# Handing on the two score banks of a windowed attention one by one, with a new weaving table, in a four-layer kernel on one Trainium2 core

## The chip, the core and the metric

One Trainium2 chip, of which the kernel uses one core. The engines are PE (TensorE: matmuls, with PEld for its weight loads), ACT (ScalarE), DVE (VectorE), POOL (GpSimd) and the DMA queues, issued from SP. Times are device microseconds of one launch; lower is better.

## The reference, cut to what matters

The input holds 8 sequences of 512 tokens and 128 channels. Each goes through four layers of the form x = x + s * silu(f), where s is an attention-like branch and f a feed-forward branch, both of the layer norm of x. Layer 1's f is the part that the change touches: a depth-2 stack in which every block does

```
q, k = l2norm(q) * qs, l2norm(k) * ksc;  q, k = rotary_xpos(q, k)
sim = where((i < j) | (i > j + 64), -big, 8 * q @ k.T)      # 8 heads of 64, window of 64
o = softmax(sim) @ v;  x = x + o @ wo
x = x + (a * gelu(g)) @ w2 + b2      # a, g from the layer norm of the shifted x
```

Layer 0 is a delta-rule scan beside a chain of small networks, layer 2 a state scan beside four experts, and layer 3 an attention whose softmax keeps the 25 largest of 512 scores in each row, found by repeated searches for the 8 largest. All arithmetic is in fp32.

## The kernel before, in words

Channels lie on the 128 partitions and tokens along the free axis. Layers 0, 1 and 2 of a sequence are one stream of work, called the item. Layer 3 of the sequence before it is a second stream, the search. The program is nine blocks: one with an item alone, seven passes of a loop in which the item of sequence b runs beside the search of sequence b-1, and one with a search alone.

Each engine has a queue that it works off in order. The four queues are written by generators that yield at the same places: the item has 200 steps, the search some 264. `weave(a, b)` merges the two: after step n of the item it puts as many steps of the search as digit n of the string `SEARCH` says (base 36). The same string orders all four engines, so it is the only scheduler; there is no dynamic one.

Steps 1 to 24 of the search set layer 3 up. Then come 32 pairs of rows of scores, 7 steps each, numbered 25 to 248, and in each of them DVE does two searches over 128x512: either two MAX8 (L2036) or two MATCH_REPLACE8 (L2040). The last 16 steps hold work of PE, ACT and POOL alone.

Layer 1's attention (the helpers `score`, `turn`, `exponent`, `take_turned`, `largest`, `share`, `divide`) has 8 units in each of the 2 blocks of the stack: unit n is 128 queries (q = n // 2) and four of the eight heads. Its scores are 4 x 192 columns in two PSUM banks, A[0] and A[1], two heads in each. A unit goes like this. PE writes the mask and the scores to both banks (`score`). DVE takes the row maxima of both in one TENSOR_REDUCE (L1189) and multiplies them by the norm of the query (L1192, "shift"). ACT computes four exponents with their sums (L1072), two from each bank. DVE takes reciprocals of the sums (L1201), and POOL multiplies the probabilities by them (L1295). PE transposes them to bank A[2], one half (e = 0, 1) at a time (`turn`, L925), and ACT copies each half out (L1083). Then PE multiplies by the values into A[3].

The units are pipelined by one: on PE, unit n's part is scores of n+1, turn of (n, 0), [at0], turn of (n, 1), [at1], values of n, [at2], where the names in brackets are the yields. On ACT it is copy of (n, 0), [at0], copy of (n, 1), the four exponents of n+1, [at1], and an output copy of every second unit, [at2]. On DVE it is maxima and shift of n+1, [at0], both reciprocals, [at1], [at2]. The scores of n+1 wait for the exponents of both banks of n, since they overwrite both.

Tables of ACT's functions are loaded where the next function in its queue needs another set (L309).

Of the kernel before, what the change touches and what calls it, by code (L numbers as in the profile page):

```python
# [8 lines left out]
ALU = mybir.AluOpType  # L9
# [194 lines left out]
class Layer:  # L204
# [9 lines left out]
    def __call__(self, name, count):  # L214
# [5 lines left out]
SEARCH = ("0030001012121031111222010302030140211310211202111220023121011011011112100401413120420311233210122111"  # L220
          "0013220130010120201016010416010130221000200144026030a2025106024101006010033015100000200010101000252")
# [11 lines left out]
def build(nc, x_in, w_in, c_in, e_in, out, wcols, ccols, ecols):  # L233
# [5 lines left out]
    with ctx:  # L239
# [420 lines left out]
        def names(*tables):  # L660
# [13 lines left out]
            PE="pj 16,px 16,mix_xc 2,mix_var 2,k 2,v 2,r 2,wo 2,ss_q 2,ss 8,vp 8,score 16,turned 32,pv 16,attn 2,gp 6,ap 6,ffn_out 2",  # L674
            ACT="hs_a 2,sqq 16,mix_sq 2,mix_ln 2,mix_rs 2,k_sb 2,sr 2,q_ln 2,q_rs 2,rn_ln 8,rn 8,vt 8,exp 32,pt 32,of 8,hs2_a 2,"
                "gelu 6,gate 1",
            DVE="t1 16,t2 16,mix_g 2,mix 2,kv 2,state 2,y 2,h 2,qk 8,qrs 2,max 16,shift 16,rec 32,x1 2,gg 6,x2 2,hs_0 1,hs_b 2,hs2_b 2,m 1,x_new 1",
# [180 lines left out]
        def l1_pe(pe):  # L858
# [45 lines left out]
            def score(i, n):  # L904
                q, f = n // 2, n % 2
                lo = 128 * q - WIN if q else 0
                n0 = 0 if q else WIN
                halves = [A[e].rearrange("p (s j) -> p s j", s=2)[:, :, n0:KW] for e in range(2)]
                for e in range(2):
                    mm(halves[e], eye[:], band[:, None, n0:KW].to_broadcast([128, 2, KW - n0]), True, False)  # L910
                for s in range(2):
                    for e in range(2):
                        g = 2 * f + s
                        r = mm(halves[e][:, s], L.qk[64 * e:64 * e + 64, g * T + 128 * q:g * T + 128 * q + 128],
                               L.qk[64 * e:64 * e + 64, (4 + g) * T + lo:(4 + g) * T + 128 * q + 128], False, s == 1)
                r.then_inc(S["score"], 1)
# [12 lines left out]
            for i in range(DEPTH):  # L929
# [31 lines left out]
                score(i, 0)  # L961
# [49 lines left out]
        def l1_act(a):  # L1011
# [21 lines left out]
            def query_root(i):  # L1033
# [3 lines left out]
                if i:  # L1037
                    a.wait_ge(*S("shift", NU * i))
# [20 lines left out]
            def exponent(i, n):  # L1059
                q, f, k = n // 2, n % 2, NU * i + n  # L1060
                n0 = 0 if q else WIN
                a.wait_ge(*S("shift", k + 1))
                if n == 0:
                    a.wait_ge(*S("zero", 2) if i == 0 else S("t3", 4 * (i + 1)))
                if k >= 2:
                    a.wait_ge(*S("turned", 2 * (k - 1)))
                    a.wait_ge(*S("rec", 2 * (k - 1)))
                table(LN, TANH)
                for e in range(2):
                    for s in range(2):  # L1070
                        j = 2 * e + s
                        r = act(L.probs[f][:, j, WIN + n0:256], A[e][:, 256 * s + n0:256 * s + KW], ACT.Exp,  # L1072
                                scale=L.qrs[:, 2 * f + s, q, e:e + 1], bias=L.shift[f][:, j:j + 1],
                                accum_out=L.zsum[f][:, j:j + 1])
                    r.then_inc(S["exp"], 1)
# [9 lines left out]
            for i in range(DEPTH):  # L1085
# [27 lines left out]
                exponent(i, 0)  # L1113
# [34 lines left out]
        def l1_dve(v):  # L1148
# [26 lines left out]
            def turn(i, n):  # L1175
# [3 lines left out]
                if n == 4 and i:  # L1179
                    v.wait_ge(*S("score", NU * i))  # L1180
                stt(L.qk[:, n * T:(n + 1) * T], L.rn[n % 2], 1e12, L.t1[n % 2], ALU.min, ALU.mult).then_inc(S["qk"], 1)

            def largest(i, n):
                q, f, k = n // 2, n % 2, NU * i + n
                n0 = 0 if q else WIN
                v.wait_ge(*S("score", k + 1))
                if k >= 2:
                    v.wait_ge(*S("exp", 2 * (k - 1)))
# [1050 lines left out]
```

## Time and profile before

| | |
|---|---|
| median of 3 runs | 5378.93 us (5370.84 to 5409.69) |
| profiled execution, its own time | 5400.17 us |
| span of the profiled execution | 5398.3 us |
| mean granted TensorE clock | 0.793 |
| DVE busy | 4012.1 us, 74% of the span |
| PE busy | 4091.9 us, 76% |
| ACT busy | 2922.0 us, 54% |
| POOL busy | 2520.7 us, 47% |
| HBM traffic | 7 GB/s |

A window of the trace is a stretch of the span, counted from its start. The row of a window gives, for each engine, how long it was busy and with how many instructions, and then the clock that TensorE was granted as a share of full speed. What is left between an engine's busy time and the length of the window is idle.

### The profile page before, as it was taken

To read this page: it belongs to the slowest core of one execution; us is meant where nothing else is said; L and a number is where in the kernel's file an instruction comes from. 1 tells how busy PE (TensorE), PEld (TensorE's weight loads), DVE (VectorE), ACT (ScalarE), POOL (GpSimd) and SP (SyncE) were. 2 spreads that over 40 slices of the span, in tenths; PEclk is the share of its full clock that TensorE was granted. 3 is DMA by queue.
4 is the path that set the end of the run, shared out by engine and by line. 5 is a ranking of instruction groups with operands and counts; after the bars stand their busy time and mean duration, and the time that the engine had idled before them with its cause. 6 is when DMAs were issued, how large, how long until landed. Compare 5 with 4: busy or idle time off the path is not lost. (4 is left out here: it accounts for less than half of the span.)

```text
span 5398.3 us, 58321 instructions
## 1 busy us (share of the span) xinstructions
PE 4091.9 (76%) x16660; PEld 1894.8 (35%) x16660; DVE 4012.1 (74%) x7871; ACT 2922.0 (54%) x5717; POOL 2520.7 (47%) x2324
## 2 busy tenths in 40 slices
PE   5776877768777787877878688786877768787676
PEld 1332334323443234422443234432344323442233
DVE  3325688876878678885787867887788867888598
ACT  3443566545555465655555465654556545565343
POOL 1114355444545345462553625545355544546265
PEclk8876898868887788968888688886898778986555
DMA  1000000000000000000000000000000000000000
GB/s 78 1 24 2 2 1 24 1 3 2 1 24 1 3 3 1 24 0 3 3 1 24 3 3 1 24 1 3 2 1 24 1 3 3 1 24 1 2 1 3
DMA packets 7995, 44.07 MB, mean 8 GB/s; under 512 B 848, under 2 KB 848, under 8 KB 7248
## 3 DMA queue, kind: packets, MB, share of 16 engines
q1 hardware_dynamic: 7632, 39.89, 1.9%
q8 instruction: 148, 2.42, 0.2%
q14 instruction: 215, 1.76, 0.1%
HBM read 37.52 MB, written 2.36 MB: 7 GB/s over the span
## 5 line engine op out<-in xcount | busy, mean ns | idle before, releaser
L2036 DVE MAX8 m<-top 128x8 f32<-128x512 f32 x2048 | 1292.5, 679 | 3.1 <-ACT top L1966 2.6
L2102 POOL TENSOR_SCALAR top<-top,m 128x512 f32<-128x512 f32 x512 | 813.6, 1589 | 959.0 <-DVE m L2036 834.4
L2040 DVE MATCH_REPLACE8 top<-m,top 128x512 f32<-128x512 f32 x1536 | 1026.1, 675 | 0.3
L288 PE MATMUL bank<-arena,consts 128*128 128x512 f32 (+1 forms) x912 | 624.7, 779 | 114.8 <-ACT arena L406 42.3
L2108 POOL TENSOR_TENSOR top<-top 128x512 f32<-128x512 f32 x512 | 656.0, 1281 | 20.2 <-ACT top L1974 2.4
L288 PE MATMUL bank<-arena,weights 128*128 128x512 f32 (+8 forms) x976 | 536.8, 669 | 87.3 <-issue 20.7
L1901 PE MATMUL bank<-consts,top 128*128 128x128 f32 x2048 | 417.6, 340 | 192.7 <-POOL top L2108 137.6
L288 PE MATMUL bank<-arena 128*64 128x128 f32 (+3 forms) x3200 | 474.5, 371 | 44.9 <-ACT arena L1083 40.2
L1901 PEld LDWEIGHTS bank<-consts,top 128*128 128x128 f32 x2048 | 303.8, 175 | 477.7 <-POOL top L2108 282.7
L1981 ACT ACTIVATE top<-bank 128x512 f32<-128x512 f32 x512 | 305.6, 597 | 298.0 <-PE bank L1901 297.4
L288 PE MATMUL bank<-top,vt 128*9 128x128 f32 x4096 | 344.0, 323 | 141.4 <-ACT top L1981 141.4
L1966 ACT ACTIVATE top<-bank 128x512 f32<-128x512 f32 x512 | 302.7, 593 | 225.4 <-PE bank L288 163.6
L1642 POOL TENSOR_TENSOR arena<-arena 128x1024 f32<-128x1024 f32 x128 | 287.0, 2242 | 210.3 <-DVE arena L1611 207.6
L309 ACT ACT_TABLE_LOAD x294 | 377.2, 1283 | 5.2
L288 PE MATMUL bank<-kf,qm 32*128 32x512 f32 x1024 | 373.6, 813 | 3.2 <-ACT top L1966 3.2
L1974 ACT ACTIVATE top<-top,nmx 128x512 f32<-128x512 f32 x512 | 365.3, 721 | 0.9
L1295 POOL TENSOR_TENSOR arena<-arena 128x384 f32<-128x384 f32 (+1 forms) x256 | 197.5, 775 | 340.9 <-DVE arena L1201 340.8
L288 PEld LDWEIGHTS bank<-arena 128*64 128x64 f32 (+2 forms) x3200 | 277.4, 181 | 215.1 <-issue 166.2
L820 POOL TENSOR_TENSOR arena<-arena,hold 128x512 f32<-128x512 f32 x64 | 83.7, 1308 | 539.2 <-DVE arena L793 539.1
L288 PE MATMUL bank<-hold,weights 128*128 128x512 f32 (+2 forms) x512 | 303.8, 725 | 24.3 <-DVE hold L427 5.6
L288 PEld LDWEIGHTS bank<-arena,consts 128*128 128x128 f32 (+1 forms) x912 | 190.8, 235 | 363.4 <-issue 134.1
L288 PEld LDWEIGHTS bank<-arena,weights 128*128 128x128 f32 (+5 forms) x976 | 175.3, 201 | 398.8 <-issue 197.1
(287 smaller groups left out, 6636.4 us busy)
## 6 DMA issues: line engine op xcount, KB each, us to landing
arena<-experts_dram SPq DMA_DIRECT2D x32, 768.0 KB, 7.1
weights<-weights_dram SPq DMA_DIRECT2D x1, 6982.0 KB, 19.2
hold<-x_dram SPq DMA_DIRECT2D x9, 256.0 KB, 2.7
out_dram<-x_out SPq DMA_DIRECT2D x9, 256.0 KB, 3.4
consts<-consts_dram SPq DMA_DIRECT2D x1, 1759.5 KB, 23.6
rot<-consts_dram SPq DMA_DIRECT2D x1, 1024.0 KB, 25.6
```

What stands on the lines that cost most here:

```text
L288: return nc.tensor.matmul(o, lhsT, rhs, start=start, stop=stop)
L309: nc.scalar.preload_act_table_set(name)
L1295: nc.gpsimd.tensor_tensor(p, p, L.rec[f][:, 2 * e:2 * e + 2, None].to_broadcast([128, 2, KW - n0]), ALU.mult).then_inc(S["shared"], 1)
L1642: nc.gpsimd.tensor_tensor(L.hc[n % 2], L.hh[n % 2], L.cn[n % 3][:, None, :].to_broadcast([128, 2, T]), ALU.mult).then_inc(S["hc"], 1)
L1901: i = nc.tensor.transpose(Y[:, 128 * k:128 * k + 128], pp[e][:, 128 * k:128 * k + 128], C("ident"))
L1966: act(sc[slot(p, e)], X[e], ACT.Copy).then_inc(SB["sc"], 1)
L1974: act(ex[e], sc[slot(p, e)], ACT.Exp, scale=SC, bias=nmx[:, slot(p, e):slot(p, e) + 1], accum_out=zs[:, q, heads[e]:heads[e] + 1]).then_in ...
L1981: act(pt_[e], Y, ACT.Copy).then_inc(SB["pt"], 1)
L2036: nc.vector.max(m8[:, slot(p, e), k], src).then_inc(SB["top"], 1)
L2040: nc.vector.match_replace(wk_[e], m8[:, slot(p, e), k], sc[slot(p, e)] if k == 0 else wk_[e], -3e38).then_inc(SB["rest"], 1)
L2102: nc.gpsimd.tensor_scalar(pp[e], sc[slot(p, e)], m8[:, slot(p, e), TOPK // 8, 0:1], None, ALU.is_ge).then_inc(SB["kept"], 1)
L2108: nc.gpsimd.tensor_tensor(pp[e], pp[e], ex[e], ALU.mult).then_inc(SB["pp"], 1)
```

## The change

Every hand-over between PE, DVE and ACT in this attention is split by bank. `score`, `largest`, `exponent` and `share` get an argument e, and the semaphores score, max and shift count 32 instead of 16. Two score matmul groups, two maxima, two shifts and two pairs of exponents take the place of one, one, one and four exponents together. A bank's scores now wait for the exponents of that bank alone, and its exponents for its own shift. The queues are reordered:

```diff
 PE:
-                        pe.wait_ge(*S("exp", 2 * k + 2))
-                        score(i, n + 1)
+                        score(i, n + 1, 0)
                     turn(i, n, 0)
                     yield "at0"
+                    if n + 1 < NU:
+                        score(i, n + 1, 1)
                     turn(i, n, 1)
                     yield "at1"
 ACT:
+                    if n + 1 < NU:
+                        exponent(i, n + 1, 0)
                     take_turned(i, n, 0)
                     yield "at0"
+                    if n + 1 < NU:
+                        exponent(i, n + 1, 1)
                     take_turned(i, n, 1)
-                    if n + 1 < NU:
-                        exponent(i, n + 1)
                     yield "at1"
 DVE:
                     if n + 1 < NU:
-                        largest(i, n + 1)
+                        largest(i, n + 1, 0)
                     yield "at0"
                     if n + 1 < NU:
-                        share(i, n + 1)
+                        share(i, n + 1, 0)
+                        largest(i, n + 1, 1)
                     yield "at1"
+                    if n + 1 < NU:
+                        share(i, n + 1, 1)
                     yield "at2"
 largest:
-                nc.vector.tensor_reduce(L.nmax[f], banks[:, 0:2].rearrange("p b (s j) -> p (b s) j", s=2)[:, :, n0:KW],
+                nc.vector.tensor_reduce(L.nmax[f][:, 2 * e:2 * e + 2], A[e].rearrange("p (s j) -> p s j", s=2)[:, :, n0:KW],
 score:
+                if n:
+                    pe.wait_ge(*S("exp", 2 * k + e - 1))
```

The matmuls, exponents, reciprocals and POOL's operations keep their shapes and counts. And the string changes as a whole:

```diff
-SEARCH = ("0030001012121031111222010302030140211310211202111220023121011011011112100401413120420311233210122111"
-          "0013220130010120201016010416010130221000200144026030a2025106024101006010033015100000200010101000252")
+SEARCH = ("0010002001010111011132020561620320302221222111023010011000003101002001201400230111110120322150031110"
+          "0230211111210121310064000451706132515220431001312252515343003223011000200000200010000100110001010221")
```

Item steps 0 to 32 are layer 0, 33 to 132 layer 1 (its two attentions are steps 48 to 73 and 96 to 121, in 8 units of at0, at1, at2 after two steps of opening), and 133 to 199 layer 2.

## Rows read from the trace of the kernel before

**Rows 1.** The page, section 1: busy time, share of the span, instructions.
```profile
PE 4091.9 (76%) x16660; PEld 1894.8 (35%) x16660; DVE 4012.1 (74%) x7871; ACT 2922.0 (54%) x5717; POOL 2520.7 (47%) x2324
```
**Rows 2.** Windows: the item alone, one loop pass, the search alone.
```profile
core 0: us, PE busy (x) PEld busy (x) DVE busy (x) ACT busy (x) POOL busy (x), PEclk, DMA share, GB/s
0.00:529.80 529.80, 360.41 (x1093) 155.69 (x1093) 199.66 (x303) 210.37 (x402) 115.67 (x99) 0.78 0.07 26
...
2455.50:3097.40 641.90, 504.87 (x2082) 235.04 (x2082) 500.78 (x981) 365.14 (x715) 315.07 (x290) 0.81 0.02 6
...
5023.10:5398.30 375.20, 244.01 (x994) 111.77 (x994) 304.95 (x701) 154.69 (x310) 197.74 (x196) 0.52 0.01 2
```
**Rows 3.** Windows: stages of that loop pass, in order.
```profile
2479.90:2565.20 85.30, 70.97 (x170) 25.14 (x168) 57.20 (x94) 53.06 (x82) 24.97 (x22) 0.90 0.00 0
...
2576.70:2623.20 46.50, 43.35 (x161) 20.38 (x160) 38.00 (x73) 27.09 (x49) 23.09 (x20) 0.89 0.00 1
2623.20:2690.70 67.50, 52.60 (x362) 31.53 (x362) 47.19 (x115) 39.65 (x116) 36.81 (x41) 0.80 0.00 1
2690.70:2717.20 26.50, 20.77 (x102) 9.58 (x102) 25.46 (x60) 16.35 (x30) 13.26 (x13) 0.94 0.00 1
...
2772.50:2837.90 65.40, 49.18 (x368) 30.71 (x366) 50.63 (x126) 40.89 (x119) 40.25 (x46) 0.87 0.00 1
2837.90:2868.30 30.40, 24.18 (x78) 10.10 (x78) 22.47 (x47) 16.76 (x27) 13.45 (x13) 0.72 0.28 104
...
2870.90:2893.60 22.70, 15.80 (x56) 7.71 (x56) 18.28 (x45) 14.62 (x23) 6.12 (x8) 0.71 0.00 0
2893.60:2974.20 80.60, 71.83 (x294) 35.04 (x294) 65.23 (x142) 43.86 (x74) 35.11 (x36) 0.89 0.00 1
2974.20:2996.90 22.70, 17.45 (x71) 7.11 (x71) 21.04 (x46) 17.46 (x34) 13.35 (x13) 0.76 0.00 0
2996.90:3084.40 87.50, 57.43 (x162) 21.23 (x161) 80.00 (x102) 41.76 (x72) 68.77 (x45) 0.58 0.00 0
```
**Rows 4.** Windows: the same stages with no search beside them (first block).
```profile
164.20:223.00 58.80, 40.01 (x246) 24.70 (x246) 11.09 (x33) 26.35 (x84) 12.38 (x16) 0.74 0.00 1
223.00:241.30 18.30, 13.29 (x22) 4.69 (x22) 4.67 (x8) 5.88 (x8) 0.00 (x0) 0.81 0.00 1
282.30:338.90 56.60, 36.93 (x246) 22.68 (x246) 11.09 (x32) 26.24 (x84) 12.38 (x16) 0.79 0.00 0
...
359.40:380.20 20.80, 12.70 (x28) 5.82 (x28) 8.24 (x21) 10.87 (x14) 0.14 (x2) 0.58 0.00 0
...
445.10:513.70 68.60, 44.48 (x62) 11.30 (x61) 58.18 (x50) 31.50 (x48) 51.20 (x29) 0.50 0.00 0
```
**Rows 5.** Timeline of one unit with no search beside it, second attention.
```profile
311.77 0.50 PE L288 MATMUL bank<-band,eye 128*128 128x384 bf16 x2 [0.88 <-ACT arena L1072]
...
313.17 0.96 DVE L1189 TENSOR_REDUCE arena<-bank 128x4 f32<-128x768 f32 x1 [1.25 <-PE bank L288]
...
314.16 0.16 DVE L1192 TENSOR_TENSOR arena<-arena 128x4 f32<-128x4 f32 x1
...
315.15 0.60 ACT L1083 ACTIVATE arena<-bank 128x512 f32<-128x512 f32 x1 [0.81 <-PE bank L925]
315.65 0.51 ACT L1072 ACTIVATE arena<-bank,arena 128x192 f32<-128x192 f32 x1
...
315.89 1.09 PE L288 MATMUL bank<-arena 128*64 128x128 f32 x16 [0.78 <-ACT arena L1083]
...
317.78 0.50 PE L288 MATMUL bank<-band,eye 128*128 128x384 bf16 x2 [0.79 <-ACT arena L1072]
```
**Rows 6.** Groups by line and form, second attention of the loop pass (2772.5:2837.9).
```profile
L2036 DVE MAX8 m<-top 128x8 f32<-128x512 f32 x36 | 22.8, 679 | 0.0
...
L1189 DVE TENSOR_REDUCE arena<-bank 128x4 f32<-128x768 f32 x6 | 5.7, 950 | 2.1 <-PE bank L288 2.1
...
L1072 ACT ACTIVATE arena<-bank,arena 128x128 f32<-128x128 f32 x8 | 3.6, 462 | 1.5 <-DVE arena L1192 1.5
...
L1189 DVE TENSOR_REDUCE arena<-bank 128x4 f32<-128x512 f32 x2 | 1.4, 678 | 0.0
```
**Rows 7.** The page, section 5: loads of ACT's function tables.
```profile
L309 ACT ACT_TABLE_LOAD x294 | 377.2, 1283 | 5.2
```

More of the change, by code:

```diff
@@ L673, in build @@
         S1 = marks.layer(**names(norm_names(("xn", False), ("ffn0", True), ("ffn1", True)), dict(
-            PE="pj 16,px 16,mix_xc 2,mix_var 2,k 2,v 2,r 2,wo 2,ss_q 2,ss 8,vp 8,score 16,turned 32,pv 16,attn 2,gp 6,ap 6,ffn_out 2",
+            PE="pj 16,px 16,mix_xc 2,mix_var 2,k 2,v 2,r 2,wo 2,ss_q 2,ss 8,vp 8,score 32,turned 32,pv 16,attn 2,gp 6,ap 6,ffn_out 2",
             ACT="hs_a 2,sqq 16,mix_sq 2,mix_ln 2,mix_rs 2,k_sb 2,sr 2,q_ln 2,q_rs 2,rn_ln 8,rn 8,vt 8,exp 32,pt 32,of 8,hs2_a 2,"
                 "gelu 6,gate 1",
-            DVE="t1 16,t2 16,mix_g 2,mix 2,kv 2,state 2,y 2,h 2,qk 8,qrs 2,max 16,shift 16,rec 32,x1 2,gg 6,x2 2,hs_0 1,hs_b 2,hs2_b 2,m 1,x_new 1",
+            DVE="t1 16,t2 16,mix_g 2,mix 2,kv 2,state 2,y 2,h 2,qk 8,qrs 2,max 32,shift 32,rec 32,x1 2,gg 6,x2 2,hs_0 1,hs_b 2,hs2_b 2,m 1,x_new 1",
             POOL="zero 2,q_sb 8,t3 8,shared 32")))
@@ L902, in value, with score @@
                 mm(A[q % 2], L.hs[:, 128 * q:128 * q + 128], W(f"l1_qkv{i}", lo=1024)).then_inc(S["vp"], 1)
-            def score(i, n):
-                q, f = n // 2, n % 2
+            def score(i, n, e):
+                q, f, k = n // 2, n % 2, NU * i + n
                 lo = 128 * q - WIN if q else 0
                 n0 = 0 if q else WIN
-                halves = [A[e].rearrange("p (s j) -> p s j", s=2)[:, :, n0:KW] for e in range(2)]
-                for e in range(2):
-                    mm(halves[e], eye[:], band[:, None, n0:KW].to_broadcast([128, 2, KW - n0]), True, False)
+                half = A[e].rearrange("p (s j) -> p s j", s=2)[:, :, n0:KW]
+                if n:
+                    pe.wait_ge(*S("exp", 2 * k + e - 1))
+                mm(half, eye[:], band[:, None, n0:KW].to_broadcast([128, 2, KW - n0]), True, False)
                 for s in range(2):
[L912 to L915, printed above, removed]
+                    g = 2 * f + s
+                    r = mm(half[:, s], L.qk[64 * e:64 * e + 64, g * T + 128 * q:g * T + 128 * q + 128],
+                           L.qk[64 * e:64 * e + 64, (4 + g) * T + lo:(4 + g) * T + 128 * q + 128], False, s == 1)
                 r.then_inc(S["score"], 1)
@@ L960, in l1_pe @@
                 pe.wait_ge(*S("qk", 4 * (i + 1)))
-                score(i, 0)
+                score(i, 0, 0)
+                score(i, 0, 1)
                 yield "hop"
@@ L1037, in query_root @@
                 if i:
-                    a.wait_ge(*S("shift", NU * i))
+                    a.wait_ge(*S("shift", 2 * NU * i))
                 act(flat, A[3][:, 0:32], ACT.Ln, scale=NORM_SCALE, bias=C("floor")).then_inc(S["q_ln"], 1)
@@ L1057, in fetch_v, with exponent @@
                 act(L.vt[:, q], A[q % 2].rearrange("p (h d) -> p h d", d=DH), ACT.Copy).then_inc(S["vt"], 1)
-            def exponent(i, n):
+            def exponent(i, n, e):
                 q, f, k = n // 2, n % 2, NU * i + n
                 n0 = 0 if q else WIN
-                a.wait_ge(*S("shift", k + 1))
+                table(LN, TANH)
+                a.wait_ge(*S("shift", 2 * k + e + 1))
                 if n == 0:
@@ L1065, in exponent @@
                 if k >= 2:
[L1066 to L1075, printed above, removed]
+                    a.wait_ge(*S("turned", 2 * (k - 2) + e + 1))
+                    a.wait_ge(*S("rec", 2 * (k - 2) + e + 1))
+                for s in range(2):
+                    j = 2 * e + s
+                    r = act(L.probs[f][:, j, WIN + n0:256], A[e][:, 256 * s + n0:256 * s + KW], ACT.Exp,
+                            scale=L.qrs[:, 2 * f + s, q, e:e + 1], bias=L.shift[f][:, j:j + 1],
+                            accum_out=L.zsum[f][:, j:j + 1])
+                r.then_inc(S["exp"], 1)
             def take_turned(i, n, e):
@@ L1232, in l1_dve @@
                 v.wait_ge(*S("qrs", i + 1))
-                largest(i, 0)
+                largest(i, 0, 0)
+                largest(i, 0, 1)
                 yield "hop"
-                share(i, 0)
+                share(i, 0, 0)
+                share(i, 0, 1)
                 yield "hop"
@@ L1282, in l1_pool @@
                             if n == 0 and i:
-                                g.wait_ge(*S("score", NU * i))
+                                g.wait_ge(*S("score", 2 * NU * i))
                             nc.gpsimd.tensor_tensor(L.qk[:, n * T:(n + 1) * T], L.t1[n % 2], L.t2[n % 2],
```

28 lines of the change are left out of this document (14 added, 14 removed).

## The prediction

> **What bounds the kernel now.** I read the page's busy times first: DVE 74% and PE 76% busy, ACT 54%, POOL 47% [rows 1]. No engine is full, so the mean says little. The windows by block say where the time is: seven loop passes of 641.9 us, 4493 of 5398 us. In one, DVE is busy 501 us, PE 505 us [rows 2]. Then I cut a pass into stages at DVE's own instructions and set the woven stages [rows 3] beside the same stages of the first block, which has no search [rows 4]. The reader is to see two kinds of stage. Some are full on DVE: the feed-forward of the first stack block (25.5 busy of 26.5 us), the state scan (80.0 of 87.5). In others DVE has room while the item's own chain runs: layer 0 (57.2 of 85.3), the two attentions (47.2 of 67.5 and 50.6 of 65.4), the experts (65.2 of 80.6) [rows 3]. The attention takes 58.8 and 56.6 us alone [rows 4], so its 29 and 31 search steps lengthen it by only 8.7 and 8.8 us: some 0.3 us for a step that keeps DVE busy for 1.28 us (my sum: 50.6 less about 12 of the attention's own, over 31; two MAX8 of 0.68 overlap a little [rows 6]). Attention is bound by its chain, and the search fills the gaps.
>
> **Part 1, the chain of a unit.** In the unit alone, at full clock, one mask matmul to the next is 317.78 - 311.77 = 6.01 us [rows 5]. It is made of scores (to the turn at about 1.3), turn, copy, turn, copy (to 315.65, when exponents start) and four exponents (2.1). The maxima end at 314.13 and the shift at 314.32, but the exponents begin at 315.65: ACT was still copying. So DVE is **not** on this loop; it has 1.33 us to spare [rows 5].
>
> Now the new order. Counting from the first mask matmul: a bank's scores end at about 0.85 (half of the group, with the pipeline's end). The maxima of one bank cover 384 columns. No row has that form; 768 columns take 0.95 and 512 take 0.678 [rows 6], a slope of 1.06 ns a column, which gives 0.54 for 384. It can't be above the 0.68 of 512 columns, and half of 0.95 is the least; I take 0.54, on the line through both forms. Shift 0.16, with hand-overs: exponents of bank 0 from 1.6 to 2.6. The copy of (n, 0) stands behind them on ACT, to 3.2. DVE's queue has the reciprocal of bank 0, which waits for these exponents, ahead of the maxima of bank 1: they run from 2.85 to 3.4, the shift to 3.55, exponents of bank 1 from 3.6 to 4.6, copy of (n, 1) to 5.2. The values (1.09 [rows 5]) wait for this copy, and on PE's queue the next scores of bank 0 stand behind the values: 5.2 + 1.1 = 6.3. So the period is about 6.25 us against 6.01: what is won by working on two banks at once is paid back, because the values, which ran beside the exponents before, are now in series, and so are maxima and shift. With PE at 1.2 GHz (the clock granted to these stages is 0.80 and 0.87 of full [rows 3], so part of the time) the same count gives 8.05, and the old order needs 8.0 by PE's groups at double length. I take **+0.25 us a unit**, between -0.1 and +0.5.
>
> DVE's own work grows by one fixed part of a maximum (0.95 becomes 2 x 0.54, +0.13) and one shift (+0.16): 0.3 us a unit, inside its idle time alone, but in the sum where DVE is full.
>
> The Trainium skill ("VectorE: DVE Perf Modes", the section on the TRN2 errata) speaks against splitting: PSUM-source operations cost 120 cycles at 0.96 GHz plus one a column, so 125 ns are paid again with each part. By the two forms above it is 0.13. In the whole program it would be 16 us by the page and 17 by the trace, of DVE's time, not of the path: 16 units in each of 8 blocks.
>
> **Part 2, the table.** I counted the digits of both strings between the item steps at which my stages begin and end; only search steps 25 to 248 hold DVE work, and both sums are 224. Steps before -> after, and the change of the stage in us, at 1.28 us of DVE a step:
> - Layer 0, 10 -> 17: 9 us of DVE into 28 idle, but in bursts of 6 at its end (digits 5, 6, 1, 6), where DVE is full. +5 (0 to 9).
> - Layer 0's end to layer 1's shift, 7 -> 5: full on DVE, -2.6. Projections, 15 -> 18, 38.0 of 46.5 busy: +2 (0 to 3.8).
> - First attention, 29 -> 21: 8 steps fewer at 0.3 to 1.28, not below 58.8 alone [rows 4]: -5; eight units of part 1, +2. Together **-3** (-8 to +2).
> - First feed-forward, 16 -> 9: DVE 25.5 - 9.0 = 16.5, alone 18.3 [rows 4], so 19.9: -6.6. The step behind it, 2 -> 1: -1.3. Second projections, 19 -> 19: 0.
> - Second attention, 31 -> 36: 5 steps at 0.3 to 1.28, +4, eight units, +2: **+6** (+1 to +9). Ten of the 36 stand in the last unit, where nothing of the attention hides them.
> - Second feed-forward, 13 -> 23: DVE 22.5 + 12.8 = 35.3, and 3 idle: +8 (5 to 12).
> - Layer 2's opening and router, 8 -> 20: DVE 18.3 + 15.4 = 33.7, and 2 idle: +13 (11 to 17).
> - Experts, 41 -> 42, and ACT's table loads in a pass: following the functions through both orders by hand I count 38 before (7 x 38 and the ends make up the 294 of [rows 7]) and 40 after, two more of these here, 1.28 us each: +1 (-5 to +5). Behind the experts, 14 -> 12: -1.5.
> - State scan, 18 -> 0: DVE 80.0 - 23.0 = 57, and alone it takes 68.6 [rows 4], which then holds it, with TensorE granted 0.50 of its clock alone and 0.58 beside the search: -18 (-19 to -15).
>
> The sum is 5 - 2.6 + 2 - 3 - 6.6 - 1.3 + 6 + 8 + 13 + 1 - 1.5 - 18 = **+2 us a pass**, +14 for seven. The first block has 16 units at 0.25: +4. The last block has no attention. So 5398.3 + 18 = 5416 of span, and the profiled execution's 5400.2 becomes 5418. That execution lies 21 us above the median, so on the median: 5379 + 18 = **5397 us**. What the sum says in plain words: the table takes the search out of a full stage (the scan) and puts it into stages that become full by it.
>
> No DMA is moved; the experts' weights are issued after the second attention as before and have 30 us.
>
> **The rivals.**
> (A) The split pays in the woven state. Alone, units cannot use more, but beside the search PE and ACT also do its matmuls and copies (PE 52.6 and ACT 39.7 busy of 67.5 [rows 3]), and smaller hand-overs let these slip between. At best DVE or PE bound the attentions: the second at 50.6 + 6.4 + 2.4 = 59.4 and little idle, 61; the first at PE's 52.6 less what 8 steps have, about 56 with hand-overs. That is 15 less instead of +3 for both, so 18 to 19 less a pass. Half of it, as is likelier, gives 5397 - 7 x 9.5 = **5330 us**; all of it 5267. For it: 20 and 15 us of idle DVE in these stages, the largest room there is. Against it: the order of part 1 puts copies behind exponents that wait for DVE.
> (B) DVE comes onto the unit's loop. Before, exponents waited 1.5 us in a whole attention for the shift [rows 6], thanks to the 1.33 us to spare. Now maxima are needed at once, and a search step that stands ahead of them delays the whole loop by up to 1.28 us, twice a unit. Half of one step a unit is 0.64 x 16 = 10 us a pass: 5397 + 72 = **5469 us**. It decides from the point where the mean wait for the shift passes some 0.6 us a unit; then the result is slower.
> (C) The stages that become full don't fill. The experts, with 41 steps, leave DVE idle for 15.4 us, 0.37 a step [rows 3]. If the 22 steps put into the second feed-forward and the router cost that on top, it is +8 a pass: **5454 us**.
> (D) The change doesn't overlap what it says, because in a woven queue the exponents of bank 0 end before the scores of bank 1 are issued anyway. Then part 1 is +0.3 of DVE work and no more; it is in the forecast's range.
>
> **How the numbers follow.** Forecast, with (D): 0.40. (A): 0.27. (B): 0.21. (C): 0.12. Within 1% (54 us, about what a measurement of this kernel can tell from no change) is the forecast alone, 0.40; faster 0.27; slower 0.33. The forecast's own range, from the bounds of the stages, is 5397 with some 6 us a pass either way, 5355 to 5440. The range of all reaches to most of (A), 5267 being its end, and past (B) and (C): 5270 to 5490.
>
> **What would show it.** Part 1: in the first block the attentions stay within 3 us of 58.8 and 56.6; (A) would have them under 55 or the woven ones at 61 and 56. Part 2: the scan near 69.5 us with TensorE granted half its clock, the router stage near 36, the second feed-forward near 38, the second attention near 71, and 294 + 14 = 308 table loads. (B): L1072 waits for L1192 for over 5 us in an attention. (C): idle DVE of over 5 us in the router and second feed-forward stages. The prediction is wrong if layer 0 loses more than 9 us to its bursts, or if the woven attentions leave the bounds of -8 to +9.

## The result and the profile after

The changed kernel takes 5614.67 us (median of 4, 5606.48 to 5644.02) against 5382.08 us before in the same comparison: a ratio of **1.043** [1.038, 1.049]. The forecast was 5397, some 18 us more than before, with a range up to 5490. The sign was right, but the loss is 233 us, thirteen times the forecast one and outside the range. The profiled span went from 5398.3 to 5604.7, 206 us more.

The page after: busy times, then three groups (the last two numbers are the idle time ahead of the group and what ended most of it).

```profile
PE 4301.8 (77%) x16660; PEld 2094.3 (37%) x16660; DVE 4035.9 (72%) x8127; ACT 2956.3 (53%) x5731; POOL 2531.5 (45%) x2324
...
L1073 ACT ACTIVATE arena<-bank,arena 128x192 f32<-128x192 f32 (+1 forms) x512 | 249.9, 493 | 488.6 <-DVE arena L1196 488.6
...
L1193 DVE TENSOR_REDUCE arena<-bank 128x2 f32<-128x384 f32 (+1 forms) x256 | 133.6, 522 | 400.5 <-PE bank L288 396.5
...
L309 ACT ACT_TABLE_LOAD x308 | 395.2, 1283 | 5.6
```

DVE and ACT do about what they did [rows 1]; the table loads are the 308 that I counted. What is new is one wait: the exponents (L1073) stand 488.6 us for DVE's shift (L1196), 3.8 us a unit over 128 units. Before, the wait was 1.5 us in a whole attention [rows 6]. PE is busy 210 us more with the same 16660 instructions.

Windows of the trace after: the first block's attentions, alone; then, from one loop pass of the changed kernel, layer 0, the first attention, second attention, second feed-forward, layer 2's opening and router, experts, scan.

```profile
165.40:241.60 76.20, 61.21 (x249) 39.64 (x248) 14.07 (x50) 26.56 (x85) 12.38 (x16) 0.53 0.00 0
304.30:379.60 75.30, 61.06 (x250) 40.16 (x248) 13.90 (x49) 26.54 (x84) 12.37 (x16) 0.52 0.00 1
...
2579.10:2678.80 99.70, 80.42 (x204) 27.88 (x203) 67.95 (x124) 56.21 (x91) 29.83 (x28) 0.87 0.00 0
...
2731.50:2810.20 78.70, 65.12 (x333) 43.15 (x332) 39.66 (x109) 36.50 (x108) 30.35 (x34) 0.65 0.00 1
...
2882.70:2977.20 94.50, 81.88 (x391) 52.57 (x390) 59.06 (x156) 45.13 (x128) 44.04 (x47) 0.58 0.00 1
2977.20:3010.70 33.50, 25.15 (x127) 11.10 (x128) 33.20 (x75) 21.04 (x36) 20.29 (x22) 0.91 0.25 95
3014.60:3049.20 34.60, 24.18 (x110) 11.81 (x108) 34.08 (x79) 21.62 (x38) 18.46 (x20) 0.70 0.00 1
3049.20:3121.80 72.60, 65.98 (x297) 33.47 (x298) 66.25 (x147) 46.88 (x76) 33.93 (x35) 0.98 0.00 1
3144.00:3215.30 71.30, 42.33 (x90) 13.81 (x91) 62.99 (x55) 33.62 (x52) 56.31 (x32) 0.64 0.00 0
```

The seven loop passes took 641.9 us each before and 665.8 after (529.8 to 5023.1, and 569.1 to 5229.4 us of the span). Cut at the same instructions and averaged over the passes:

```
stage                        before   after   change   forecast
layer 0                        86.2   101.1    +14.9       +5
layer 0's end                  11.5     7.6     -3.9       -2.6
projections, first             46.5    45.9     -0.6       +2
first attention                64.6    80.2    +15.6       -3
first feed-forward + step      29.6    23.6     -6.0       -7.9
projections, second            52.3    48.8     -3.5        0
second attention               65.2    86.2    +21.0       +6
second feed-forward            28.2    33.4     +5.2       +8
layer 2's opening, router      21.5    34.7    +13.2      +13
experts                        80.6    72.5     -8.1       +1
behind the experts             22.6    20.6     -2.0       -1.5
scan                           87.5    71.4    -16.1      -18
the rest                       45.6    39.8     -5.8        -
```

The two attentions give 36.6 us more a pass, everything else together 12.7 less. Alone, with no search and so no table in play, they went from 58.8 and 56.6 [rows 4] to 76.2 and 75.3. So at least that part has nothing to do with the search steps.

The timeline of one unit alone, after (start, length, instruction, then the idle time before it and its releaser), set beside [rows 5]:

```profile
320.17 0.50 PE L288 MATMUL bank<-band,eye 128*128 128x384 bf16 x1
...
320.60 1.65 PE L288 MATMUL bank<-arena 64*128 64x192 f32 x4
...
322.18 1.11 PE L925 MATMUL bank<-consts,arena 128*128 128x128 f32 x4
322.28 0.56 DVE L1193 TENSOR_REDUCE arena<-bank 128x2 f32<-128x384 f32 x1 [3.30 <-PE bank L288]
...
323.07 0.51 ACT L1073 ACTIVATE arena<-bank,arena 128x192 f32<-128x192 f32 x1 [2.19 <-DVE arena L1196]
323.08 0.53 PE L288 MATMUL bank<-band,eye 128*128 128x384 bf16 x1
...
323.54 1.65 PE L288 MATMUL bank<-arena 64*128 64x192 f32 x4
...
325.12 1.12 PE L925 MATMUL bank<-consts,arena 128*128 128x128 f32 x4
325.22 0.56 DVE L1193 TENSOR_REDUCE arena<-bank 128x2 f32<-128x384 f32 x1 [0.86 <-PE bank L288]
...
326.01 0.51 ACT L1073 ACTIVATE arena<-bank,arena 128x192 f32<-128x192 f32 x1 [1.36 <-DVE arena L1196]
...
327.00 0.59 ACT L1084 ACTIVATE arena<-bank 128x512 f32<-128x512 f32 x1
...
327.74 1.98 PE L288 MATMUL bank<-arena 128*64 128x128 f32 x16 [1.50 <-ACT arena L1084]
...
329.65 0.50 PE L288 MATMUL bank<-band,eye 128*128 128x384 bf16 x1
```

From mask to mask it is 9.48 us (320.17 to 329.65), and the rows are one chain: bank 0's scores and the turn behind them on PE (2.91), bank 1's mask and scores (2.14), maxima and shift (0.79), two exponents (0.99), the copy (0.74), the values (1.91). Read the copy: its input, the second turn, was done at 325.12 + 1.12 = 326.24, but it starts at 327.00, behind exponents that had themselves waited for DVE until 326.01. PE idles 1.50 us for it, then does the values, and the next scores stand behind these. DVE's reciprocal isn't a link of this chain: DVE has done it and then idles 0.86 us until PE has written bank 1. The Trainium skill ("TensorE: Matmul & The Clock Gate", "Architectural detail: the array is 16× 32×32, not 1× 128×128") calls ACT and DVE strictly first in, first out; the row agrees, a copy whose data was there did not pass the exponents. The mask takes 0.50 us for one bank, as two banks took in [rows 5]: this unit runs at 1.2 GHz. The windows of these attentions are granted 0.53 and 0.52, where it was 0.74 and 0.79 [rows 4].

### The profile page after: what moved, and what is told of

Read it like the earlier page. It is cut to its first block and busy times, and to the rows that moved or that the text cites. A ratio compares the mean times of both kernels' runs of the same rounds, so it can differ in the third digit from the quotient of the medians.

```text
span 5604.7 us, 58831 instructions
## 1 busy us (share of the span) xinstructions
PE 4301.8 (77%) x16660; PEld 2094.3 (37%) x16660; DVE 4035.9 (72%) x8127; ACT 2956.3 (53%) x5731; POOL 2531.5 (45%) x2324
## 5 line engine op out<-in xcount | busy, mean ns | idle before, releaser
L288 PE MATMUL bank<-arena 128*64 128x128 f32 (+3 forms) x3200 | 727.7, 444 | 142.3 <-ACT arena L1084 142.3
L288 PE MATMUL bank<-arena,consts 128*128 128x512 f32 (+1 forms) x912 | 611.1, 763 | 94.5 <-POOL arena L1650 27.3
L288 PEld LDWEIGHTS bank<-arena 128*64 128x64 f32 (+2 forms) x3200 | 463.3, 224 | 348.0 <-issue 262.7
L1073 ACT ACTIVATE arena<-bank,arena 128x192 f32<-128x192 f32 (+1 forms) x512 | 249.9, 493 | 488.6 <-DVE arena L1196 488.6
L1193 DVE TENSOR_REDUCE arena<-bank 128x2 f32<-128x384 f32 (+1 forms) x256 | 133.6, 522 | 400.5 <-PE bank L288 396.5
L288 PE MATMUL bank<-hold,weights 128*128 128x512 f32 (+2 forms) x512 | 271.7, 656 | 81.2 <-DVE hold L643 26.2
```

The costliest lines, as they stand in the source:

```text
L288: return nc.tensor.matmul(o, lhsT, rhs, start=start, stop=stop)
```

## The experiments

Three theories. **Q**: the queue orders put copies and maxima behind exponents, so that one long loop forms through ACT, DVE and PE. **P**: PE's scores lose the pairing of the two row halves when each bank is written by itself. **T**: the new table. Later **K**: TensorE's lower clock is a loss of its own. The first four kernels take P and T.

**Scores in bank order, kernel before.**

```diff
-                for s in range(2):
-                    for e in range(2):
+                for e in range(2):
+                    for s in range(2):
```


> The kernel before, and only the order of a unit's eight score matmuls is changed: all of bank 0 (rows 0 to 63 of the array), then all of bank 1 (rows 64 to 127), where they alternated. Theory P (matmuls of the two row halves ran two at a time, and the change undid that): a unit's 8 row-tiled score instructions take about 3.3 us at half clock instead of 1.65, the attentions of the first block go from 58.8 and 56.6 us to 70 to 76, TensorE's clock in them falls towards 0.5, and the time rises by 3 to 4%, to some 5570 us. Theory O (the new queue order costs: values, maxima and shift in series): no change, 5382 within 0.5%, since no queue order between engines is touched. Theory T (the new table costs): no change either.

Measured: 5389.35 us, 1.002 [1.0006, 1.0034]; attentions alone 56.5 and 55.8. The timeline of this kernel shows why:

```profile
311.49 0.93 PE L288 MATMUL bank<-arena 64*128 64x192 f32 x8
```

All eight score instructions still take 0.93 us; in the trace those of the two halves start 13 to 14 ns apart (the first two at 311.491 and 311.505), though four of one half stand ahead of four of the other in the queue. The order inside a group costs nothing as long as both banks are there.

**Both banks' scores issued together, in the changed kernel** (its other edits kept).

```diff
-                        score(i, n + 1, 0)
+                        score(i, n + 1)          # both banks, halves alternating
                     turn(i, n, 0)
                     yield "at0"
-                    if n + 1 < NU:
-                        score(i, n + 1, 1)
```


> The changed kernel, but the scores of both banks of a unit are issued together again, alternating between the row halves, when the exponents of both banks before are done; maxima, shifts, exponents and reciprocals stay split by bank, in the new order, with the new table. Theory P: the attentions of the first block return to 59 to 64 us (the split's own order costs 0.25 us a unit), their clock to 0.7 to 0.8, and the time is 5330 (5280 to 5400) us, 1% under the kernel before, since the new table outside the attentions saves 12 us a pass. Theory O: the attentions stay at 72 to 76 us alone and the time above 5520. Theory T: above 5500.

Measured: 5617.03, 1.045 [1.0428, 1.0472]; attentions alone 73.8 and 73.7. PE's busy time in them fell from 61 to 47 us, and the time stayed: P is real work for PE and not the cause. What holds the chain changed: a unit takes 9.11 us at half clock (313.60 to 322.71), and now the second maxima start at 318.03, right behind the reciprocal at 317.95, with both banks' scores done since 316.

**The two tables, crossed** (the string alone is exchanged): the changed kernel with the old string, and the kernel before with the new one.

> The changed kernel with the old weaving table. Theory P: the attentions alone are the same as with the new table (76 and 75 us) and the time is no better than the changed kernel's, 5640 to 5720 us, because the stages outside the attentions lose the 12 us a pass that the new table gave. Theory T: the loss goes away, under 5450 us.

> The kernel before with the new weaving table: only the digits change. Theory P with my reading of the stages: woven attentions at about 60 and 70 us, the rest of a pass at 500, so 630 us a pass instead of 642 and 5300 us (5250 to 5360) in all, faster than the kernel before by 1.5%. Theory T: slower than before, above 5450 us.

Measured: 5675.52, 1.055 [1.0521, 1.0576], and 5393.1, 1.0022 [1.0004, 1.004]. T falls too: with the old attention the new table makes a pass of 641.3 us against 641.9. It moves time (layer 0 +13, router +14, scan -16, experts -8) and saves none. In the changed kernel it softens the loss by 61 us. The difference lies in the woven attentions: with the old attention the table makes the two 8.2 us a pass longer (64.6 and 65.2 become 68.3 and 69.7), with the changed one 2.9 us shorter (84.3 and 85.1 become 80.2 and 86.2).

**The split alone.** The hand-overs are split by bank as in the change; the queues keep the old order (both maxima, both reciprocals; both copies, then the four exponents; both banks' scores together), old table.

```diff
 ACT:
                     take_turned(i, n, 1)
                     if n + 1 < NU:
-                        exponent(i, n + 1)
+                        exponent(i, n + 1, 0)
+                        exponent(i, n + 1, 1)
 DVE:
-                        largest(i, n + 1)
+                        largest(i, n + 1, 0)
+                        largest(i, n + 1, 1)
                     yield "at0"
-                        share(i, n + 1)
+                        share(i, n + 1, 0)
+                        share(i, n + 1, 1)
```


> The kernel before, old table, with only the hand-overs split by bank: maxima, shifts, exponents and reciprocals of a bank each, with semaphores of their own, but every queue in the order of before (both maxima; copy, copy, four exponents; both reciprocals) and the scores of both banks issued together. Theory Q (what costs is the new order of the queues, exponents ahead of copies): 5382 us within 0.7%, attentions of the first block at 56 to 60 us. Rival S (the split itself costs, by more and smaller instructions and more semaphores): attentions over 64 us alone, time above 5430 us.

Measured: 5389.45, 1.001 [0.9997, 1.0022]; alone 57.2 and 58.8. The finer semaphores, 128 more maxima and as many shifts cost nothing that shows.

**The changed kernel with one swap on ACT**, new table.

```diff
-                        exponent(i, n + 1, 0)
                     take_turned(i, n, 0)
+                        exponent(i, n + 1, 0)
                     yield "at0"
-                        exponent(i, n + 1, 1)
                     take_turned(i, n, 1)
+                        exponent(i, n + 1, 1)
```


> The changed kernel, new table, with one change to ACT's queue: in each half of a unit the copy of the turned probabilities stands ahead of the exponents of the next unit's bank instead of behind them. Theory Q: the second copy no longer waits for the second bank's exponents, so the values follow it 1.5 to 2 us earlier; attentions of the first block fall from 76 and 75 to 62 to 68 us and the time to 5400 (5350 to 5480) us. Rival S, or DVE's order (reciprocal ahead of the second maxima) as the cause: attentions stay over 72, time above 5560.

Measured: 5393.28, 1.002 [1.0009, 1.0032]. Two lines moved on one queue take back 221 of the 233 us. What is left is the time of the new table with the old attention (5393.1), and the woven attentions are at its level too, 68.9 and 69.5 us. Alone it is another matter: the attentions of the first block take 68.0 and 66.8, still 19 us more together than with the old attention and this table (57.1 and 58.8). The equal totals come about because a pass is some 3 us shorter (638.8 against 641.7 us from attention to attention); why isn't shown. The group of the exponents, the window of the first attention alone, and the copy in its timeline, of this kernel:

```profile
L1073 ACT ACTIVATE arena<-bank,arena 128x192 f32<-128x192 f32 (+1 forms) x512 | 249.1, 494 | 60.9 <-DVE arena L1196 60.7
```
```profile
164.10:232.10 68.00, 59.36 (x249) 39.00 (x248) 14.24 (x48) 26.64 (x84) 12.36 (x16) 0.55 0.00 0
```
```profile
317.37 1.11 PE L925 MATMUL bank<-consts,arena 128*128 128x128 f32 x4
...
318.52 0.60 ACT L1084 ACTIVATE arena<-bank 128x512 f32<-128x512 f32 x1 [1.36 <-PE bank L925]
319.01 0.51 ACT L1073 ACTIVATE arena<-bank,arena 128x192 f32<-128x192 f32 x1
...
319.17 1.97 PE L288 MATMUL bank<-arena 128*64 128x128 f32 x16 [0.69 <-ACT arena L1084]
```

The copy starts as the turn ends (318.48), and values and exponents run side by side, 319.17 beside 319.01. The wait for the shift is 60.9 us in place of 488.6.

**ACT's order alone, and DVE's order alone**, each added to the split kernel above, old table. 
```diff
 ACT alone:
+                        exponent(i, n + 1, 0)
                     take_turned(i, n, 0)
                     yield "at0"
+                        exponent(i, n + 1, 1)
                     take_turned(i, n, 1)
-                        exponent(i, n + 1, 0)
-                        exponent(i, n + 1, 1)
 DVE alone:
                         largest(i, n + 1, 0)
-                        largest(i, n + 1, 1)
                     yield "at0"
                         share(i, n + 1, 0)
-                        share(i, n + 1, 1)
+                        largest(i, n + 1, 1)
                     yield "at1"
+                        share(i, n + 1, 1)
```

> Before with the hand-overs split by bank and the old table, as in the split with old queue order; the only further edit is ACT's order: exponents of (n+1, 0) ahead of the copy of (n, 0), exponents of (n+1, 1) ahead of the copy of (n, 1). DVE keeps both maxima ahead of both reciprocals, PE issues both banks' scores together. Theory Q (the copies stand behind exponents that wait for the shift): nearly all of the loss of the change with the old table (5676 us) is here, 5620 to 5690, attentions alone 72 to 77 us. Rival (DVE's order, the reciprocal ahead of the second maximum, makes the chain): with DVE's order left as it was the time stays at 5385 to 5430, attentions alone under 62. If both are needed: half, about 5530, attentions alone near 67.

> The same split kernel with the old table; the only further edit is DVE's order: maxima of (n+1, 0), then the reciprocal of (n+1, 0) ahead of the maxima of (n+1, 1), then the reciprocal of (n+1, 1). ACT keeps both copies ahead of the four exponents. Theory Q: the second maximum now waits for the first pair of exponents, which stand behind both copies, so the second shift and exponents follow a little later: 58 to 62 us for an attention alone, 5390 to 5440 in all. Rival (DVE's order makes the chain): 5600 or more, attentions alone over 70.

Measured: **5523.1**, 1.0259 [1.0239, 1.028], alone 68.1 and 66.2; and **5641.95**, 1.0482 [1.0463, 1.0502], alone 72.7 and 74.0. The first lands where I had written that both would be needed, the second where the rival had it. So neither theory stands alone: ACT's order, which I had made the whole cause, costs 141 us by itself, and DVE's order, which I took for harmless, 260 when ACT keeps its old one. The timeline of the second, ACT and DVE in one unit:

```profile
321.67 0.60 ACT L1084 ACTIVATE arena<-bank 128x512 f32<-128x512 f32 x1 [1.27 <-PE bank L928]
322.16 0.51 ACT L1073 ACTIVATE arena<-bank,arena 128x192 f32<-128x192 f32 x1
...
324.41 0.51 ACT L1073 ACTIVATE arena<-bank,arena 128x192 f32<-128x192 f32 x1 [1.16 <-DVE arena L1195]
```
```profile
319.35 0.16 DVE L1195 TENSOR_TENSOR arena<-arena 128x2 f32<-128x2 f32 x1
323.28 0.17 DVE L1203 RECIPROCAL arena<-arena 128x2 f32<-128x2 f32 x1 [3.78 <-ACT arena L1073]
323.37 0.55 DVE L1192 TENSOR_REDUCE arena<-bank 128x2 f32<-128x384 f32 x1
```

DVE has nothing to do from 319.51 to 323.28, while bank 1's scores lie ready. Its queue holds a reciprocal, which needs bank 0's exponents, which stand behind both copies on ACT. So exponents of bank 0, reciprocal, maxima, shift and exponents of bank 1 come one after the other. The changed kernel has both reversals, but not both on its chain: in its unit above PE's second scores come after the reciprocal, so ACT's order and PE's hold it. When PE writes both banks together, the reciprocal takes that place. In the kernel with ACT's lines swapped DVE's order is the changed one as well, and the woven attentions don't suffer from it. So the 141 and the 260 us are prices of each order beside the old order of the others; they don't add up, and both orders with the scores apart cost 295 (5675.5 against 5380.3). PE's order alone wasn't run.

**Everything in the order in which it becomes ready**, old table: on ACT copy 0, exponents 0, copy 1, exponents 1; on DVE both maxima, then the reciprocals; both banks' scores together.

```diff
 ACT, against the split kernel:
                     take_turned(i, n, 0)
+                        exponent(i, n + 1, 0)
                     yield "at0"
                     take_turned(i, n, 1)
-                        exponent(i, n + 1, 0)
                         exponent(i, n + 1, 1)
```
DVE's second reciprocal also stands one yield later, behind "at1".

> Old table, scores of both banks issued together, both maxima first on DVE, then on ACT copy of half 0, exponents of bank 0, copy of half 1, exponents of bank 1. Theory Q: exponents of bank 0 fill the 0.8 us in which ACT waited for the second turn, and the values run beside the exponents of bank 1: period 5.5 us at full clock instead of 6.0, attentions of the first block 54 to 56 us, time 5320 (5270 to 5370) us. Rival S: 5400 to 5450 us.

Measured: 5353.92, **0.9943** [0.9924, 0.9962]: the split does pay a little, once nothing stands in front of its gain. Alone the attentions take 53.9 and 51.3 us, under the 58.8 and 56.6 of before; woven 63.9 and 66.2, as before (64.6 and 65.2). A unit takes 5.12 us at full clock in place of 6.01, but 7.9 to 8.0 at half clock, as before. So 10 of the 31 us against the kernel before in this comparison (5385.36) are located, in the first block. In the passes the largest difference stands behind the attention, not in it: the second feed-forward takes 24.5 us in place of 28.2 (26.4 in the split kernel with the old order). Why isn't shown, and the share of each stage is uncertain, since a woven attention of the kernel before varies from 60.3 to 67.6 us between the passes of one execution. Its windows alone:

```profile
165.10:219.00 53.90, 38.97 (x246) 24.32 (x246) 13.20 (x49) 26.07 (x84) 12.36 (x16) 0.75 0.00 1
275.40:326.70 51.30, 35.52 (x246) 22.24 (x246) 13.22 (x49) 25.96 (x84) 12.36 (x16) 0.83 0.00 1
```

**Filler for TensorE.** The changed kernel, with eight mask matmuls of 192 columns into a free bank behind each unit's second turn, in the first block alone; they are extra work, and no output depends on them.

```diff
                     turn(i, n, 1)
                     yield "at1"
+                    if fill[0]:
+                        for _ in range(8):
+                            mm(X[0][:, 0:192], eye[:], band[:])
```


> The changed kernel with eight extra mask matmuls of 192 columns a unit into an unused PSUM bank, in the first block only, where TensorE would wait for the second copy. Theory K (part of the loss is TensorE's clock, granted 0.53 in the attentions of the first block against 0.74 and 0.79 before, because it idles more): the clock there rises above 0.75 and the attentions fall from 76 and 75 to 64 to 70 us although work is added; the loop passes are unchanged. Without K: 76 to 84 us, as the added work lengthens the queue.

Measured (one run, 5578.21): the first block's attentions went from 76.2 and 75.3 to 64.7 and 61.2, and the loop passes, which have no fillers, stayed within 1%. The windows of this kernel:

```profile
163.30:228.00 64.70, 54.92 (x314) 38.51 (x312) 14.26 (x49) 26.52 (x84) 12.36 (x16) 0.74 0.00 1
285.80:347.00 61.20, 47.25 (x314) 33.44 (x312) 14.92 (x50) 26.54 (x85) 12.37 (x16) 0.86 0.00 1
```

With more to do, PE is granted 0.74 and 0.86 in place of 0.53 and 0.52, and is done sooner. K holds, in these two stages, by one run. One comparison is at the same mean clock: the first attention takes 64.7 us at 0.74 against 58.8 at 0.74 before [rows 4], so about 6 of its 17.4 us are the order's and the rest is the clock's.

What keeps the clock low isn't shown. It is not more idle time of PE in sum: with ACT's two lines swapped PE idles 8.6 of 68.0 us and is granted 0.55, where before it idled 18.8 of 58.8 and was granted 0.74 [rows 4]. (PE's busy time is itself longer at the low clock.) The three kernels with the banks' scores apart and no fillers are at 0.52 to 0.57 alone, those with them together at 0.56 to 0.83.

The same timeline gives the changed order's period at full clock:

```profile
321.38 0.34 PE L288 MATMUL bank<-band,eye 128*128 128x384 bf16 x1
...
323.24 0.91 PE L288 MATMUL bank<-arena 64*128 64x192 f32 x4
...
324.51 0.17 DVE L1208 RECIPROCAL arena<-arena 128x2 f32<-128x2 f32 x1 [1.16 <-ACT arena L1077]
324.59 0.55 DVE L1197 TENSOR_REDUCE arena<-bank 128x2 f32<-128x384 f32 x1
...
325.18 0.42 DVE L1200 TENSOR_TENSOR arena<-arena 128x2 f32<-128x2 f32 x1
...
325.57 0.82 PE L288 MATMUL bank<-band,eye 128*128 128x192 bf16 x8
...
327.26 1.09 PE L288 MATMUL bank<-arena 128*64 128x128 f32 x16 [0.87 <-ACT arena L1088]
...
328.29 0.34 PE L288 MATMUL bank<-band,eye 128*128 128x384 bf16 x1
```

It is 6.91 us (321.38 to 328.29). The fillers end at 326.39, 0.87 us before the values start, so they aren't on the chain. At full clock bank 1's scores end at 324.15, ahead of the reciprocal at 324.51: here DVE's order is the link.

**A joined table**: the old digits for item steps 0 to 121, the new ones behind (digit 125 made 1), in the kernel before and in the kernel with everything in order.

```diff
-          "0013220130010120201016010416010130221000200144026030a2025106024101006010033015100000200010101000252")
+          "0013220130010120201016000151706132515220431001312252515343003223011000200000200010000100110001010221")
```

> Before, with a string joined from both: digits 0 to 121 of the old one, the rest of the new one (digit 125 made 1 instead of 4, so that the search stands where the new string has it). If each stage costs what its own digits make it cost (local theory): from the second feed-forward to the end of the pass the changed kernel took 242.5 us against 252.8 before, 10.3 less a pass, so 5385 - 72 = 5313 us; with the opening of the next pass (16.3 against 11.4) 5279. Rival (what is won behind is given back in front, as with the whole new table, which gave 5393): 5375 to 5400.

> The version with the exponents of a bank between the two copies and both maxima first (5354 us with the old table), now with the joined string. By the local theory the two gains add: 5354 - 72 = 5282 us, 5250 to 5290 with the next pass's opening. Rival (the tail's gain goes, as with the whole new table): 5345 to 5365.

Measured: 5354.96, 0.9946 [0.9927, 0.9964], and 5346.17, 0.9931 [0.9913, 0.9948]. The first lies between the local theory (5313) and its rival (5375 or more), the second where its rival had it. The tail's stages came out as cheap as in the changed kernel (scan 72.2 and 71.7, experts 72.5 both), but the second feed-forward took 37.2 and 34.6 us, where its neighbours with the old table take 28.2 and 24.5: it loses 9 and 10 us a pass, where the changed kernel had lost 5.2. Of 72 us expected, 27 and 8 arrive. The second has the lowest time of the study, 0.7% under the kernel before, which is less than the 1% that I set as the bound; its interval overlaps that of its neighbour with the old table.

All orders of the attention in one table (times alone are of the first block; the period of a unit is read from mask to mask at half clock):

```
ACT's order          DVE's order             table   us       alone        period
copies, exponents    maxima, reciprocals     old     5389.5   57.2, 58.8   8.0
exponents first      maxima, reciprocals     old     5523.1   68.1, 66.2   8.6
copies, exponents    reciprocal 0 between    old     5642.0   72.7, 74.0   9.2
exponents first      reciprocal 0 between    old     5675.5   74.8, 75.4   9.5
exponents first      reciprocal 0 between    new     5614.7   76.2, 75.3   9.5
bank by bank         reciprocal 0 between    new     5393.3   68.0, 66.8   8.7
bank by bank         maxima, reciprocals     old     5353.9   53.9, 51.3   7.9
```

Here "exponents first" is the change's order on ACT, "bank by bank" copy 0, exponents 0, copy 1, exponents 1. Rows 4 to 6 also have the scores of the banks apart on PE.

## Why the prediction was wrong

**The step that failed is Part 1's unit, +0.25 us "between -0.1 and +0.5".** The queue orders that it read were right, and so was the sentence that values, maxima and shift are now in series. The length was not.
- At half clock my count gave 8.05 for the new order and 8.0 for the old. The old one is 8.0 in the trace (rows below). The new one is 9.48: +1.48, not +0.05. At full clock it is 6.91 against 6.01 [rows 5] and my 6.25: +0.90, not +0.25.
- The term that was too small is a bank's scores, which I let end "at about 0.85", with half of the group. A bank's four instructions take 1.65 us at half clock, as all eight did before, and 0.91 at full. The first bank's scores are done 1.21 us behind the start of the mask at full clock (DVE starts at 322.59) and 2.11 at half, where the count has 0.85 and, at doubled length, 1.7.
- What comes second depends on the clock. At half clock I had the second maximum start when the reciprocal was done; it starts when PE has written bank 1 (0.86 us idle, ended by PE), and these scores stand behind the turn of (n, 0) on PE, a queue that my count walked past. The 0.4 us of the first bank and the 0.9 us of this wait are nearly all of the 1.43 between count and trace. At full clock the count's chain through the reciprocal is the real one, and the other 0.26 us is the second shift: 0.42 us in place of 0.16. It ends at 325.60, with POOL's multiplication (324.75 to 325.58).
- I took the clock of the stages as given, 0.74 to 0.87. The changed order left TensorE at 0.53. Alone, 11.5 and 14.1 of the 17.4 and 18.7 us that the attentions lost came back with fillers. How much of the woven loss is clock wasn't tried; their granted clock fell from 0.80 and 0.87 [rows 3] to 0.65 and 0.58, and stands at 0.73 and 0.83 with ACT's two lines swapped. It isn't all clock: with DVE's order alone the first attention of a pass took 79.1 us at 0.76.

```profile
296.97 0.82 PE L288 MATMUL bank<-band,eye 128*128 128x384 bf16 x2 [0.86 <-ACT arena L1072]
...
297.73 1.65 PE L288 MATMUL bank<-arena 64*128 64x192 f32 x8
...
304.97 0.82 PE L288 MATMUL bank<-band,eye 128*128 128x384 bf16 x2
```

**The woven attentions** left "the bounds of -8 to +9". With the old table in both kernels they get 19.6 and 19.9 us longer, 2.5 a unit; with the new table in both, 11.9 and 16.5, 1.8 a unit. I had units cost the same woven as alone; that was right in kind, since 16 units alone lose 36 us, 2.3 each. The number carried over was wrong, not the carrying. A second term was wrong there: 8 search steps fewer in the first attention were to bring -5, at 0.3 to 1.28 us a step. With the old attention the first attention went from 64.6 to 68.3 us instead. The second, with 5 steps more, came as forecast (+4.5 for +4). So the number of steps alone doesn't price an attention.

**Part 2's sum held, by errors that cancel.** With the old attention the table is -0.6 us a pass; I had +2, with +4 of it Part 1's, so -2 for the table. The full stages came within 3 us of the forecast: scan, router, second feed-forward, first feed-forward. Layer 0 loses 15 instead of "+5 (0 to 9)": in the window above the item is 8 us ahead of the kernel before at its last scan (L793, 59 us in) and loses 22 us in what follows. There DVE is idle 14 of 20 us and then busy 19.7 of the last 19.8: the burst of digits stands behind the idle time and can't use it. Experts gain 8 instead of losing 1: I priced table loads there, though the loads (right in number) don't hold that stage; why it gains isn't shown.

**The rivals.** (B) named the sign that came, L1072's wait for the shift over 5 us in an attention, as the groups of the second attention in the pass above show:

```profile
L1073 ACT ACTIVATE arena<-bank,arena 128x192 f32<-128x192 f32 x24 | 12.1, 506 | 30.9 <-DVE arena L1196 30.9
...
L1193 DVE TENSOR_REDUCE arena<-bank 128x2 f32<-128x384 f32 x12 | 6.7, 558 | 28.2 <-PE bank L288 28.1
```

But its mechanism, a search step ahead of the maxima, is not it: DVE is idle ahead of the maxima for 28.2 us and waits for PE. The loop is closed by the orders, alone as well as woven, and (B)'s 5469 was too low by 146. (A) is refuted for this order. In the order of readiness the split does pay 0.6%, but not as (A) had it: the attentions are shorter alone and about the same beside the search. (C) fails: DVE is idle for 0.5 of 34.6 us in the router and 0.3 of 33.5 in the second feed-forward. (D) fails too: alone, bank 1's mask is issued at 323.08, just as bank 0's exponents start (323.07), and the unit costs far more than 0.3.

The price of splitting a maximum was right: 557 ns for 384 columns, where I took 0.54; the split kernel shows that DVE had the room for it.

## What to carry over

When a hand-over is split, walk every queue once with the question "is this instruction's input ready later than its follower's?", and put each queue in the order in which inputs become ready; two such inversions here cost 141 and 260 us alone, and mending the one on ACT takes back nearly all in the passes, and less than half of what the attentions lose alone. Do this count for each engine's queue in turn, PE's too, at both clocks, and take a group's length from a row of that very group, since half the instructions may take the whole time. A changed order can leave TensorE at a lower clock and so pay twice: look at the granted clock of the stage before and after.

## What the hardware showed that I had not expected

- Four 64-row matmul instructions of one half take as long as eight of both halves: 1.65 us for x4 and for x8 at half clock, 0.91 and 0.93 at full. And the pairs form even with the halves one after the other in the queue (13 to 14 ns apart). The Trainium skill ("TensorE: Matmul & The Clock Gate", Part 3 on packing small matmuls) has work of different row groups overlap; the rows agree, and show that alternating the halves isn't needed for it here.
- Work added to TensorE made a stage shorter: 75.3 us at 0.52 of the clock, 61.2 at 0.86 with 64 instructions more.
- The shift, 0.16 us alone, takes 0.42 us when it runs beside POOL's multiplication (325.18 in the timeline with fillers), and ends within 0.02 us of it. With DVE's order alone it is the same: 323.95 to 324.37, beside POOL from 323.53 to 324.36.
